# Cross-attention in a decoder layer: the reciprocal of the softmax sums ahead of the next mask addition in VectorE's order

## The reference, cut to what matters

```python
x = x + _L0_xattn_ref(_layernorm(x), ctx_1024, ctx_1024, mask_SxS2_bk0, Wq, Wk, Wv, Wo)

def _L0_xattn_ref(q, k, v, mask, Wq, Wk, Wv, Wo):      # q: 2 x 2048 x 512, k = v: 2 x 128 x 512
    q_i, k_i, v_i = (heads(t @ W) for ...)             # 16 heads of 64
    s_qk = einsum('...hik,...hjk->...hij', q_i, k_i) / sqrt(64)
    s_qk = where(mask, s_qk, -finfo.max)
    attn = softmax(s_qk, axis=-1)                      # over the 128 keys
    vals = einsum('...hij,...hjv->...hiv', attn, v_i)
    return merge_heads(vals) @ Wo
```

## Time and profile before

| | us |
|---|---|
| median of 3 runs | 3370.57 |
| lowest and highest | 3363.94, 3373.97 |
| profiled execution, span | 3371.7 |
| PE busy | 2970.8 (88%) |
| DVE busy | 2267.0 (67%) |
| ACT busy | 1607.3 (48%) |
| POOL busy | 1250.4 (37%) |

### The profile page before, as it was taken

The page is one execution under the profiler, slowest core; times in us unless marked ns, Lnnn a source line. Parts: engine busy times, 40 slices in busy tenths (PEclk is TensorE's granted clock), DMA queues, the critical chain, the costliest instruction groups (busy, mean ns, idle before and its releaser), DMA issues. The chain is left out here.

```text
span 3371.7 us, 46176 instructions
## 1 busy us (share of the span) xinstructions
PE 2970.8 (88%) x13559; PEld 2361.0 (70%) x13561; DVE 2267.0 (67%) x2504; ACT 1607.3 (48%) x2696; POOL 1250.4 (37%) x701
## 2 busy tenths in 40 slices
PE   5788888888957999999869999999198999999997
PEld 3566666666746777777757888888176777777775
DVE  7989999999866555555443333333777775766777
ACT  3556666666645555555421111111166663655664
POOL 2455555555231111111100000000467674766776
PEclk8999999999988999999979999999599999999999
DMA  3100000000031111111031111111377774767774
GB/s 116 47 20 19 19 19 19 19 19 19 13 126 34 38 37 50 38 38 38 26 121 52 58 50 50 50 59 50 136 258 268 246 259 154 252 211 243 249 255 160
DMA packets 189383, 331.62 MB, mean 98 GB/s; under 512 B 23144, under 2 KB 41576, under 8 KB 189312
## 3 DMA queue, kind: packets, MB, share of 16 engines
q1 hardware_dynamic: 177520, 304.48, 27.0%
q0 software_dynamic: 11792, 26.25, 2.3%
HBM read 295.76 MB, written 46.66 MB: 102 GB/s over the span
## 5 line engine op out<-in xcount | busy, mean ns | idle before, releaser
L1407 DVE TENSOR_TENSOR e_wL<-e_raw,e_wH 128x1024 fp32r<-128x1024 f32 x248 | 458.8, 1869 | 56.6 <-ACT e_wH L1402 54.2
L321 DVE TENSOR_TENSOR a_p<-a_r 128x1024 f32<-128x1024 f32 x256 | 436.5, 1713 | 57.4 <-ACT a_r L200 57.1
L177 POOL TENSOR_TENSOR a_pL<-a_p,a_pH 128x1024 fp32r<-128x1024 f32 x96 | 254.8, 2655 | 444.5 <-DVE a_p L321 426.9
L200 ACT ACTIVATE a_r<-a_pS 128x1024 f32<-128x1024 f32 x256 | 263.0, 1027 | 324.4 <-PE a_pS L49 318.0
L1407 POOL TENSOR_TENSOR e_wL<-e_raw,e_wH 128x1024 fp32r<-128x1024 f32 x136 | 388.9, 2879 | 36.6 <-ACT e_wH L1402 23.1
L1402 ACT CAST e_wH<-e_raw 128x1024 fp32r<-128x1024 f32 x322 | 327.0, 1050 | 63.9 <-DMA e_raw<-in_L_ffn_routed_up_w 32.5
L705 POOL TENSOR_TENSOR b_S<-b_S,b_ri 128x1024 f32<-128x1024 f32 x64 | 121.5, 1899 | 558.4 <-DVE b_ri L802 558.4
L47 PE MATMUL a_pO<-a_pH,a_vH 128*128 128x512 f32 x512 | 217.4, 425 | 106.6 <-POOL a_pL L177 99.4
L326 DVE TENSOR_TENSOR a_pL<-a_p,a_pH 128x1024 fp32r<-128x1024 f32 x160 | 296.6, 1854 | 17.1 <-DVE a_p L321 0.5
L200 ACT ACTIVATE a_pH<-a_r 128x1024 fp32r<-128x1024 f32 x256 | 271.6, 1061 | 11.9
L1261 POOL MEMSET r_ones<- 128x128 bf16 x1 | 0.2, 205 | 658.6 <-POOLq L970 658.6
(11 more groups left out here) (292 smaller groups left out, 7911.0 us busy)
## 6 DMA issues: line engine op xcount, KB each, us to landing
e_raw<-in_L_ffn_routed_gate_w SPq DMA_DIRECT2D x256, 256.0 KB, 3.6
e_raw<-in_L_ffn_routed_up_w SPq DMA_DIRECT2D x256, 256.0 KB, 4.6
e_raw<-in_L_ffn_routed_down_w SPq DMA_DIRECT2D x128, 512.0 KB
a_xg<-in_x SPq DMA_DIRECT2D x8, 1024.0 KB, 5.4
a_xb<-in_x SPq DMA_DIRECT2D x32, 256.0 KB, 2.7
x<-a_o SPq DMA_DIRECT2D x32, 256.0 KB, 2.2
b_xb<-x SPq DMA_DIRECT2D x32, 256.0 KB, 2.7
b_xr<-x SPq DMA_DIRECT2D x32, 256.0 KB, 3.2
```

Source lines behind the costliest of these rows:

```text
L177: nc.gpsimd.tensor_tensor(pL[:, c % 4, :, :], p[:, c % 2, :, :], pH[:, c % 4, :, :].bitcast(F32), ALU.subtract).then_inc(s["lowP"], 1)
L200: return nc.scalar.activation(out, in_, func)
L321: nc.vector.tensor_tensor(p[:, c % 2, :, :], r[:, c % 2, :, :], r[:, c % 2, :, :], ALU.mult).then_inc(s["p"], 1)
L1407: unit.tensor_tensor(self.wL[:, n, :, :], self.raw[:, n, :, :], self.wH[:, n, :, :].bitcast(self.F32), self.sub).then_inc(self.low_count(n ...
```

## The change

On VectorE `inverse(n - 1)` stands in front of `add_mask(n)`, for all steps but the very first, which has no pair before it.

```diff
                 def body(g, b, pb, first, last):
                     for j in range(NPAIR):
                         n = NPAIR * g + j
-                        add_mask(n, g, j)
                         if j or not first:
                             inverse(n - 1, (j - 1) % NPAIR)
+                        add_mask(n, g, j)
                         maximum(n, j)
                         if j < NPAIR - 1:
                             q_low(n + 1, j + 1)
```

## The result

| | before | with the change |
|---|---|---|
| median, us (14 runs each) | 3368.26 | 3381.15 |
| lowest and highest | 3361.37, 3378.57 | 3377.57, 3389.39 |
| profiled execution: span | 3371.7 | 3379.5 |
| cross-attention, first to last multiplication of POOL | 632.0 | 641.6 |
| routed experts, first to last matmul into `d_pG` | 910.3 | 915.9 |

The ratio is 1.004, 95% interval [1.0031, 1.0048]: 13 us slower where 2 us faster was forecast, and outside the range. The stage between is noise: the kernel before, profiled a second time, took 597.9 us there, with the cross-attention at 632.0 and the routed experts at 910.3 again. So in these two traces the change added 9.6 us to the cross-attention and, which the prediction did not ask about, 5.6 us to a stage that begins some 760 us later.

What follows compares the result with a forecast made beforehand. PE was taken to set the pace, busy 77.79 of 83.60 us. Seven turns at -0.32 (-2.2) and +0.4 in the last group gave -1.8 us, so 3368.8 us, range 3361 to 3378.

Steps and rivals of the forecast that it cites:

- q_low is now E + 0.15 + 0.45 (b_bias) + 1.25 + ...: Step j = 0, VectorE: q_low counted from the pair's last accumulator read (E), making the scores of j = 1 0.2 later.
- "Net 0" for j = 0: Step j = 0: POOL starts 0.43 earlier, the next scores 0.2 later; no net change in PE's lag.
- the lag is absorbed: Step j = 1: the scores' 0.2 delay disappears because the transposes wait for POOL anyway.
- The price that no row showed: Mask addition running beside POOL's multiplication: taken as 0, at most 1.90 us a step if it stood still throughout.
- I take 0: Cost assumed for the mask addition beside POOL, from q_low's 0.68 us beside POOL's 1.90 us.
- Rival 2: Plain steps: mask addition and maximum lengthen the softmax loop; fully exposed about +44, 3415 us; chance 0.07.
- forecast 83.2: Cross-attention: the period of one group was to become 83.2 us instead of 83.5.
- forecast -1.8: Whole kernel: -0.32 a turn for 7 groups, -2.2, and +0.4 in the last group, sum -1.8 us.
- The hand-off from the reciprocal in plain steps: VectorE, reciprocal to next instruction: 0.12 by the row; 0.20 by the skill's rule would add about 2 us in all.
- handed back: Step j = 7: the reciprocal ahead of b_xL returns 0.37 of the 0.69 gained at j = 5, leaving -0.32.
- Rival 3, the clock: Query matmuls at j = 7 run at 1.2 GHz after PE's longer wait: 2.4 a turn, +15 us, 3386; chance 0.04.
- The stages around it keep their work and order: nothing for them: Stages outside the cross-attention: no change in time, since their work and order stay.

## Why the prediction was wrong

The sum of the parts, for the changed kernel in its first trace: what was forecast -2.0 (read below), `b_bias` held +9.0 (5 x (9.14 - 7.35)), one slow query +1.3, and +1.4 once at step j = 1. There the scores and the beginning of the next query, behind the 2.15 that the stall makes TensorE wait, ran at the 1.2 GHz level (granted clock 0.64 in 1097.0 to 1101.5), and POOL's next multiplication came after 28.98 instead of 27.55. That makes 9.7 of the 9.6 measured. In the second trace the first two parts alone make 7.0 of 6.8. With the routed experts, +5.6 and +9.5, the two traces come to about 15 and 16, against 12.9 between the medians; the stage between, which took 605.2 and 597.9 in two traces of one kernel, leaves such a gap room.

- **"q_low is now E + 0.15 + 0.45 (b_bias) + 1.25 + ...", "Net 0" for j = 0: this is the step that failed.** 0.45 was read while POOL stood idle, and the change moves the instruction to 0.10 behind POOL's start. It is 2.12 from there to the mask addition, and the hand-off ahead of it 0.38 and not 0.12. The scores of j = 1 wait 2.15. And "the lag is absorbed" is untrue for a lag of that size: all of it reaches the period, 85.0 and not 83.2.
- The price that no row showed was named for the right reason and for the wrong instruction. The mask addition reads one operand from PSUM and is not held, 1184 ns; "I take 0" was right for it. Rival 2 did not happen.
- The rest came out. In the group without the stall the period was 83.1, forecast 83.2. Where the changed kernel is cured of the stall and its slow queries are taken off (635.8, less 5.8 for four of them), cross is 630.0: -2.0, forecast -1.8. The hand-off from the reciprocal in plain steps was 0.12, as by the row and not 0.20. The Trainium skill ("VectorE: DVE Perf Modes", section "The DRAIN you can't avoid"), which the prediction cites for the 0.20, also says there that a next instruction that is not held starts earlier, so page and trace need not differ. In a plain step the reciprocal starts 0.03 behind its data and the mask addition 0.12 behind it; at j = 5 the transposes' wait went from 1.03 to 0.16; PE at j = 7 waits longer for b_xL (1.85 instead of 1.53), the gain "handed back":

```profile
1568.06 0.19 ACT L723 ACTIVATION_READ_ACCUMULATOR b_S<-b_S,b_nm 128x1 f32 x1
```
```profile
1568.28 0.20 DVE L802 RECIPROCAL b_ri<-b_rs 128x8 f32<-128x8 f32 x1 [1.08 <-ACT b_S L723]
1568.40 1.18 DVE L792 TENSOR_TENSOR b_S<-b_pS,b_bias 128x1024 f32<-128x1024 f32 x1
1569.62 1.22 DVE L798 TENSOR_REDUCE b_nm<-b_S 128x8 f32<-128x1024 f32 x1
```
```profile
1407.63 1.09 PE L902 MATMUL b_pT<-ident,b_S 128*128 128x128 f32 x8 [0.16 <-POOL b_S L705]
```

- Rival 3, the clock, had 0.04 because at a turn of before "the slow matmuls lay in a wait". True there; with the new order at j = 7 they lay in the query in 26 of 63 turns, at 1.2 to 1.9 us each. It forecast 2.4 a turn.
- "The stages around it keep their work and order: nothing for them" failed by 5.6 us. Their work was the same; a race between DVE and POOL, won by 0.03 us, was lost. What delays DVE by a tenth there stays open.

## What to carry to other kernels

Before an instruction of VectorE is put behind a signal that also releases GpSimd, look at each instruction behind that signal for the kind that GpSimd can hold (here a `tensor_scalar` from SBUF to SBUF, or two SBUF inputs), and at the register work ahead of it, which decides who starts first: it must run during the wait, not behind it. Keep what doesn't wait for the signal ahead of it, as the mask's values were. Then look for the steps that really are late: here one of eight had all of the gain (cross -3.8 with j = 5 alone, one slow query included, and -4.1 with six steps), and the new order in those six steps beats both kernels. And a difference of 5 us on a kernel of 3370 can come from a few instructions more or less on one engine, so a change that alters the length of a program wants a control that only does that.

## What was not expected of the hardware

- Two memsets more in VectorE's program made a stage that begins over 700 us later 4 to 6 us longer, in both traces (914.5 and 916.0 against 910.3 twice). Two engines that started within 0.14 us of each other, and which of them was first, made the difference.
- Behind two waits of TensorE, one of 1.87 us and one of 0.5 to 1.9 us, up to nine matmuls of the query ran at the 1.2 GHz level in some executions and at none of the turns in others of the same kernel; six useless matmuls in the second wait kept the query at 2.4 GHz and made the program 6 and 13 us faster by the ratios.
- Three register instructions behind a waiting one cost 0.26 us (0.38 instead of 0.12 to the next instruction). Ahead of the wait two of them had cost nothing: in the kernel before, `b_bias` starts 1.14 behind the start of b_tL in looped code, with them between, and 1.14 in unrolled code, without.
